# Block 0's retrieval made token-major by accumulating products, its first expert products cut by token halves, and the last block's second memory layer put among the experts

## The reference, cut to what matters

```python
# x: 2048 tokens (8 x 256) of 128 features
def lmm(params, h):                        # the memory, two layers
    for W, b in params:
        h = h + silu(h @ W + b)
    return h
# attention part: gradients of a weighted squared error of lmm(keys) against values,
# one Adam-like step on W1, b1, W2, b2, then the retrieval with the new parameters
new = adamw(params, grads)
retrieved = lmm(new, queries)
x = x + layernorm(retrieved)
# expert part: z = layernorm(layernorm(x)) * g + b; logits = z @ rW + rb; top 2 of 8, softmax over them
hid   = gelu(z @ W1[e] + b1[e])            # 128 -> 256, exact gelu
mixed = sum_e w[e] * (hid @ W2[e] + b2[e])
x = x + layernorm(layernorm(x) + mixed)
```

## Time and profile before

| | us |
|---|---|
| median of three runs | 188.84 |
| lowest, highest | 187.68, 188.96 |
| the profiled execution, device time | 187.79 |
| its span | 186.0 |
| TensorE products busy, of the span | 168.9 |
| VectorE busy | 137.1 |
| ScalarE busy | 95.4 |
| GpSimd busy | 25.2 |

### The profile page before, as it was taken

One profiled execution on the slowest core, in us unless ns is written; L12 is line 12 of the kernel. 1 busy time (PEld: TensorE's weight loads), 2 busy tenths in 40 slices (PEclk: granted clock), 3 DMA queues, 4 the chain that ended last, 5 costly groups with the idle time before them and its releaser, 6 DMA issues.

```text
span 186.0 us, 3109 instructions
## 1 busy us (share of the span) xinstructions
PE 168.9 (91%) x1036; PEld 136.4 (73%) x1036; DVE 137.1 (74%) x541; ACT 95.4 (51%) x165; POOL 25.2 (14%) x36
## 2 busy tenths in 40 slices
PE   6589999998999798996999999999999999999950
PEld 6334455666655367995999998998999998989940
DVE  0989998997766828399356979866979775458574
ACT  3059776765575597242725435725426725346300
POOL 1450000000031700024000025100026000002011
PEclk9999999999999999999999999999999999999995
DMA  4991000000000000000000000100000100000101
GB/s 140 310 314 42 5 4 0 0 0 2 4 0 0 0 0 2 4 0 0 0 4 0 2 0 4 56 0 0 5 0 0 59 2 0 0 4 2 56 0 56
DMA packets 3423, 4.99 MB, mean 27 GB/s; under 512 B 336, under 2 KB 1744, under 8 KB 3408
## 3 DMA queue, kind: packets, MB, share of 16 engines
q1 hardware_dynamic: 3408, 4.81, 8.2%
HBM read 3.76 MB, written 1.05 MB: 26 GB/s over the span
## 4 chain that ended last, share of the span: by engine, by line
PE 72%; DVE 17%; ACT 3%; issue 2%; DMA 2%; POOL 1%; SPq 0%; DVEq 0%; ACTq 0%
PE bank L372 66%; PE bank L380 4%; DVE stats L831 3%; DMA x_tok<-in_x_dram 2%; DVE xnT L1083 2%; DVE mv L834 1%; DVE xn_tok L988 1%; PE bank L525 1%; DVE xn_tok L844 1%; PE bank L516 1%; DVE h_tok L844 1%; ACT L753 1%; DVE xnT L1094 1%; DVE xnT L1114 1%; DVE xnT L1066 1%
## 5 line engine op out<-in xcount | busy, mean ns | idle before, releaser
L1083 DVE SCALAR_TENSOR_TENSOR xnT<-bank,w_tok,xnT 128x128 f32<-128x128 f32 x124 | 34.9, 345 | 24.4 <-PE bank L372 23.8
L325 POOL TENSOR_TENSOR rstd<-vpe,minus_half 128x4 f32<-128x4 f32 (+1 forms) x24 | 21.8, 913 | 116.5 <-DVE vpe L839 105.3
L372 PE MATMUL bank<-z_hi,fW_hi 128*128 128x512 f32 x64 | 27.8, 434 | 0.3 <-ACT alrT L649 0.3
L372 PE MATMUL bank<-z_hi,fW_lo 128*128 128x512 f32 x64 | 25.0, 390 | 0.0
L372 PE MATMUL bank<-z_lo,fW_hi 128*128 128x512 f32 x64 | 25.0, 393 | 0.0
L372 PEld LDWEIGHTS bank<-fW_sb,sig 128*128 128x128 f32 x192 | 23.0, 192 | 0.7
L372 PE MATMUL bank<-fW_sb,sig 128*128 128x128 f32 x192 | 23.2, 275 | 0.0
L772 ACT ACTIVATE sig<-bank,early_sb 128x512 f32<-128x512 f32 x24 | 16.1, 687 | 10.5 <-PE bank L372 10.4
L372 PEld LDWEIGHTS bank<-fW_sb,k_tok 128*128 128x128 f32 x160 | 19.4, 191 | 0.8
L372 PEld LDWEIGHTS bank<-fW_sb,h1T 128*128 128x128 f32 x160 | 19.4, 191 | 0.8
L372 PE MATMUL bank<-fW_sb,k_tok 128*128 128x128 f32 x160 | 19.5, 275 | 0.0
(11 more groups left out here) (128 smaller groups left out, 266.9 us busy)
## 6 DMA issues: line engine op xcount, KB each, us to landing
x_tok<-in_x_dram SPq DMA_DIRECT2D x4, 256.0 KB, 4.3
fW_raw<-in_fW_dram SPq DMA_DIRECT2D x1, 1024.0 KB, 9.8
out_dram<-xn_tok SPq DMA_DIRECT2D x3, 256.0 KB, 2.5
early_sb<-in_early_dram SPq DMA_DIRECT2D x1, 268.0 KB, 3.8
late_sb<-in_late_dram SPq DMA_DIRECT2D x1, 264.0 KB, 4.7
b_raw<-in_late_dram SPq DMA_DIRECT2D x16, 4.0 KB
out_dram<-xn_tok SPq DMA_DIRECT2D x2, 128.0 KB, 1.9
fW_sb<-in_fW_dram SPq DMA_DIRECT2D x1, 0.5 KB, 12.1
```

What stands on the lines that cost most here:

```text
L325: pool.tensor_tensor(rstd[:, ln, where], vpe[:, ln, where], minus_half[:, 0:where.stop - where.start], ALU.pow).then_inc(rstd_ready[ln], 1)
L372: return pe.matmul(out_, lhsT, rhs, start=start, stop=stop)
L1083: last = dve.scalar_tensor_tensor(out=y_tok[:, t, :], in0=bank[Y_BANK[m % len(Y_BANK)]][:, i * P:(i + 1) * P], scalar=w_tok[:, t, e:e + 1] ...
```

## The change

1. The Silu table is loaded by a dummy activation ahead of ScalarE's copy k(3), in the learning part, and no longer behind it.
2. Block 0 (pieces 0 and 1): no `retrieved_sum` and no transposes. `token_major_hidden` multiplies each tile of h1, as the stationary operand, with the identity into `R_BANK`, and `token_major_rest` adds the tile of s2 in the same way.
3. The rz products wait for qT block by block, rz1(2) is done in two halves, and the order on TensorE and ScalarE is another. `rz2_rest(3)` stands inside `first_hidden`.
4. `first_hidden` makes three hidden products (n = 0, 1, 2) in place of two, each by token halves: the z_hi products of the first half wait for the first half of z_hi only. All six z_lo products come behind.
5. The last piece's rz2 is one product, in slot 6 behind `output(6)`, in bank 4; its silu is made in slot 7 on ScalarE by x/2 (Identity) and tanh(x/2), which come from the Gelu table's set, and a product on VectorE (`last_product`) in slot 15. `hidden_sum(3)` and `(4)` move to slot 3.
6. `w_transpose(0)` stands behind `output(0)`, no longer ahead of it.
7. neg_shift and the L1 variance step leave `residual` for `residual_rest`, behind both `norm_z` of block 0 and directly behind `residual` of the later blocks. GpSimd does LZ of piece 1 ahead of L1 of piece 0.

```diff
-        RZ1, RZ2 = (3, 5, 7, 5, 6), (6, 2, 3, 2, 6)
-        R_BANK, Z_BANK = (4, 0, 4, 4, 4), (7, 1, 7, 7, 7)
+        RZ1, RZ2 = (3, 5, 7, 5, 6), (6, 2, 3, 2, 4)
+        R_BANK, Z_BANK = (4, 0, 4, 4, 4), (7, 6, 7, 7, 7)
+        HIDDEN_SUM, LAST_RZ2, LAST_TANH = 3, 6, 7
...
             piece_rsqrt(LZ, 0)
+            piece_rsqrt(LZ, 1)
             piece_rsqrt(L1, 0)
-            piece_rsqrt(LZ, 1)
...
+            def token_major_hidden(p):
+                pe.wait_ge(rh1_done, p + 1)
+                for i, t in enumerate(piece_tiles(p)):
+                    mm(bank[R_BANK[p]][:, i * P:(i + 1) * P], r_h1T[:, t * P:(t + 1) * P], ident[:],
+                       start=(i == 0), stop=False)
+
+            def token_major_rest(p):
+                pe.wait_ge(rs2_ready, p + 1)
+                for i, t in enumerate(piece_tiles(p)):
+                    last = mm(bank[R_BANK[p]][:, i * P:(i + 1) * P], r_s2[:, t * P:(t + 1) * P], ident[:],
+                              start=False, stop=(i == HALF - 1))
+                last.then_inc(r_tr, 1)
...
             rz1_product(1)
-            rz1_product(2)
+            rz1_part(2, slice(0, HALF * P), False)
             rz2_product(0)
+            token_major_hidden(0)
             rz2_product(1)
+            token_major_rest(0)
+            token_major_hidden(1)
+            token_major_rest(1)
+            rz1_part(2, slice(HALF * P, BLOCK), True)
+            rz1_product(3)
             rz2_query(2)
-            r_transpose(0)
-            r_transpose(1)
-            rz1_product(3)
+            rz2_rest(2)
             rz1_product(4)
+            z_transpose(0)
             rz2_query(3)
-            rz2_rest(2)
-            rz2_rest(3)
-            z_transpose(0)
-            rz2_query(4)
             z_transpose(1)
-            rz2_rest(4)
...
             def first_hidden():
+                halves = [slice(h * HALF * P, (h + 1) * HALF * P) for h in range(2)]
                 pe.wait_ge(x1_ready, 2)
...
+                for h, where in enumerate(halves):
+                    pe.wait_ge(zhi_done, h + 1)
+                    for n in range(len(H_BANK)):
+                        if h == 0 and n == 2:
+                            pe.wait_ge(rs1_ready, 4)
+                        s = slice(n * P, (n + 1) * P)
+                        mm(bank[H_BANK[n]][:, where], fW1_hi[:, s], z_hi[:, where], start=(h == 0), stop=False)
+                        mm(bank[H_BANK[n]][:, where], fW1_lo[:, s], z_hi[:, where], start=False, stop=False)
+                rz2_rest(3)
+                for h, where in enumerate(halves):
+                    pe.wait_ge(zlo_done, h + 1)
+                    for n in range(len(H_BANK)):
+                        last = mm(bank[H_BANK[n]][:, where], fW1_hi[:, n * P:(n + 1) * P], z_lo[:, where],
+                                  start=False, stop=(h == 1))
+                        if h:
+                            last.then_inc(h_mm, 1)
...
                 if slot == 0:
-                    w_transpose(0)
                     pe.wait_ge(fw2_in, 16)
-                    pe.wait_ge(rs2_ready, len(RETRIEVED))
+                    pe.wait_ge(rs2_ready, 4)
+                    pe.wait_ge(zT_ready, 2)
...
                 if slot >= 0:
                     output(slot)
+                if slot == 0:
+                    w_transpose(0)
+                if slot == LAST_RZ2:
+                    rz2_product(len(RETRIEVED) - 1)
...
+                    if (what, b) == ("k", NB - 1):
+                        act.activation(warm[:], minus_half[:, 0:1], ACT.Silu).then_inc(table_ready, 1)
...
-            act.activation(warm[:], minus_half[:, 0:1], ACT.Silu).then_inc(table_ready, 1)
+            def last_silu():
+                p = len(RETRIEVED) - 1
+                act.wait_ge(rz2_mm, p + 1)
+                act.wait_ge(half_bias, 1)
+                act.activation(nsig1[:, 0:BLOCK], bank[RZ2[p]][:], ACT.Identity, scale=0.5,
+                               bias=bn_half[:]).then_inc(halved, 1)
+                act.activation(nsig2[:, 0:BLOCK], bank[RZ2[p]][:], ACT.Tanh, scale=0.5,
+                               bias=bn_half[:]).then_inc(tanh_ready, 1)
+
...
             silu1(3)
+            silu2(2)
             silu1(4)
-            silu2(2)
-            silu2(3)
             zT_out(0)
             zT_out(1)
-            silu2(4)
+            silu2(3)
...
+            def last_product():
+                dve.wait_ge(halved, 1)
+                dve.wait_ge(tanh_ready, 1)
+                dve.scalar_tensor_tensor(out=piece(r_s2, len(RETRIEVED) - 1), in0=nsig2[:, 0:BLOCK], scalar=1.0,
+                                         in1=nsig1[:, 0:BLOCK], op0=ALU.add, op1=ALU.mult).then_inc(last_s2_done, 1)
...
+            def residual_rest(p):
+                where = piece_span(p)
+                plus_eps(L1, where)
                 dve.scalar_tensor_tensor(out=neg_shift[:, where], in0=mv[:, LR_, where, 0], scalar=-1.0,
                                          in1=rstd[:, LR_, where], op0=ALU.mult,
                                          op1=ALU.mult).then_inc(shift_ready, 1)
...
             hidden_sum(1)
-            retrieved_sum(0)
-            retrieved_sum(1)
...
             norm_z(1)
+            residual_rest(0)
+            residual_rest(1)
...
+                if slot == HIDDEN_SUM:
+                    half_of_bias()
+                    hidden_sum(3)
+                    hidden_sum(4)
```

More of the change, by code:

```diff
@@ L139, in memory_and_experts @@
         bn = sb("bn", [P, 2])
+        bn_half = sb("bn_half", [P, 1])
         stats = sb("stats", [P, T, 6])
@@ L190, in memory_and_experts @@
             "shift_ready", "centred", "lg_read", "dp_done"))
+        half_bias, halved, tanh_ready, last_s2_done = (sem(n) for n in (
+            "half_bias", "halved", "tanh_ready", "last_s2_done"))
         h_mm, g_done, y_mm, b2_mm, init_done, acc_done, yn_done = (sem(n) for n in (
@@ L478, in _, with rz1_part @@
                         steps[what](b)
-            def rz1_product(p):
+            def rz1_part(p, where, last):
                 if p == 0:
                     pe.wait_ge(w1n_ready, 1)
-                pe.wait_ge(qT_ready, NB)
+                pe.wait_ge(qT_ready, max(p, 1))
                 if p == 3:
@@ L488, in rz1_product @@
                     pe.wait_ge(rs2_ready, 1)
-                mm(bank[RZ1[p]][:, 0:piece_width(p)], w1n[:], piece(qT, p)).then_inc(rz1_mm, 1)
+                ins = mm(bank[RZ1[p]][:, where], w1n[:], piece(qT, p)[:, where])
+                if last:
+                    ins.then_inc(rz1_mm, 1)
+            def rz1_product(p):
+                rz1_part(p, slice(0, piece_width(p)), True)
             def rz2_product(p):
@@ L494, in rz2_product @@
                     pe.wait_ge(dh1_done, NB)
+                if p == 1:
+                    pe.wait_ge(qT_ready, NB)
+                if p == 4:
+                    pe.wait_ge(lg_read, 2)
                 pe.wait_ge(rh1_done, p + 1)
@@ L520, in z_transpose @@
                 pe.wait_ge(zt_ready, p + 1)
+                if p == 1:
+                    pe.wait_ge(rs1_ready, 5)
                 if p >= 2:
@@ L580, in hidden @@
                     pe.wait_ge(zlo_done, j + 2)
-                if n == C:
-                    pe.wait_ge(rs1_ready, 4)
                 if n >= len(H_BANK):
@@ L623, in _ @@
                 elif slot + AHEAD < STEPS:
-                    for c in range(C):
-                        hidden(C * (slot + AHEAD) + c)
+                    for n in range(C * (slot + AHEAD), C * (slot + AHEAD) + C):
+                        if n >= len(H_BANK):
+                            hidden(n)
                 if slot == 0:
-                    w_transpose(0)
                     pe.wait_ge(fw2_in, 16)
-                    pe.wait_ge(rs2_ready, len(RETRIEVED))
+                    pe.wait_ge(rs2_ready, 4)
+                    pe.wait_ge(zT_ready, 2)
                 if slot == 1:
@@ L788, in _ @@
                     gate_tanh(0)
+                if slot == LAST_TANH:
+                    last_silu()
                 if slot == 0:
@@ L991, in residual @@
                 last.then_inc(x1_ready, 1)
-                dve.scalar_tensor_tensor(out=neg_shift[:, where], in0=mv[:, LR_, where, 0], scalar=-1.0,
-                                         in1=rstd[:, LR_, where], op0=ALU.mult,
-                                         op1=ALU.mult).then_inc(shift_ready, 1)
                 yield
@@ L1001, in residual @@
                                   ALU.mult, ALU.add).then_inc(vpe_ready[LZ], 1)
+            def residual_rest(p):
+                where = piece_span(p)
                 plus_eps(L1, where)
+                dve.scalar_tensor_tensor(out=neg_shift[:, where], in0=mv[:, LR_, where, 0], scalar=-1.0,
+                                         in1=rstd[:, LR_, where], op0=ALU.mult,
+                                         op1=ALU.mult).then_inc(shift_ready, 1)
             def norm_z(p):
@@ L1139, in _ @@
```

(13 more changed lines are left out.)

16 lines of the change are left out of this document (10 added, 6 removed).

## The result

The changed kernel takes 0.7% longer than the one before: ratio 1.007, 95% interval 1.0048 to 1.0092. The medians of twenty executions each are 189.79 us (188.56 to 191.56) and 187.89 us (187.56 to 190.16), 1.0% apart; the ratio is one of means and leaves out executions that are more than 1.5% above the fastest of their kernel, here the one of 191.56. Both kernels' times stand in clusters, and the mean granted TensorE clock that each execution lists tells them apart.

| mean granted clock | executions | median us |
|---|---|---|
| 0.988 and more | 8 | 188.6 |
| 0.979 to 0.982 | 11 | 190.1 |
| 0.969 | 1 | 191.6 |

What follows compares the result with a forecast made beforehand. From 87 us TensorE's unbroken product list was taken to bound the kernel. Slot 1's -0.49, +0.07 for neg_shift and +0.86 for rz2_product(4) gave +0.44 us, 188.8 counted from 188.3; range 187.2 to 190.3.

Steps and rivals of the forecast that it cites:

- Silu load in its gap, at no price: Ahead of k(3)'s copy on ScalarE: load and dummy, 1.40 us, fit a 1.68 us idle gap and cost nothing.
- Rival D: Slower: the Silu load misses its gap and delays k(3)'s copy by 1.40 us; 190.1 us, chance 0.08.
- hidden_sum(0) at 55.35, rz2(0) at 55.93: Start of block 0's retrieval: silu1(0) starts 0.65 us earlier, then hidden_sum(0) at 55.35, rz2(0) at 55.93, silu2(0) at 56.63.
- Token-major products: Block 0's retrieval: transposes and two VectorE sums go, eight products come; VectorE's statistics start at 57.97, 0.82 us earlier.
- The decisive step, rz2_rest(3) ahead of the Gelu load: First expert products: silu2(3) waits for rz2_rest(3), first Gelu 0.64 us later, TensorE idle 1.5 us; 0.6 of 2.3 us lead left.
- The bound that I put behind it, retrieved_sum(2): Before slot 1: r_transpose(2) needs retrieved_sum(2), ending 74.32, so TensorE comes at 74.45; rival B has it hold r_transpose(2) too.
- rival B: Faster: the Gelu gate doesn't hold TensorE; slot 1 starts 1.15 us earlier, total -0.2, 188.1 us, chance 0.15.
- rz2_product(4) paid in full: Unbroken product list: rz2_product(4), two records of 0.43, adds 0.86 us with nothing to hide it.
- The wait for norm_z(2) stays, the rest is hidden: Block 1's z transposes: TensorE's 1.8 us wait moves along unchanged; added ScalarE steps and later sums cost nothing.
- slot 1's -0.49: After block 0's retrieval and first expert products: slot 1 starts 0.49 us earlier than in the kernel before.
- Rival C, the clock: Slower: waits of 0.98 and 1.5 us within 8 us lower TensorE's clock; +0.44 + 3.2, 191.9 us, chance 0.07.

Runs made afterwards that it cites:

- run 2: Changed kernel with GpSimd's two output-bias steps moved behind z_low(1): 188.2 us at a full clock, ratio 1.0060 to the kernel before.
- run 9: Kernel before with dummy transposes in two early TensorE waits, plus only the Silu load moved ahead of k(3)'s copy: 187.7 us, ratio 0.9987 to the kernel before.
- run 10: Kernel before with early dummy transposes, Silu load moved and GpSimd's bias steps behind z_low(1): 187.1 us at a full clock, ratio 0.9995 to the kernel before.
- run 4: Changed kernel with rz2_query(3) ahead of z_transpose(0) and rz2_rest(3) between the z transposes, out of first_hidden: 187.0 us at a full clock, ratio 0.9971 to the kernel before.
- run 5: Changed kernel with the last piece's rz2 as query and rest in slot 3, its silu in slot 4: 187.85 us at a full clock, ratio 0.9991 to the kernel before.
- run 8: Changed kernel with dummy transposes in the early TensorE waits and 12 in the wait for the first Gelu: 189.1 us, ratio 1.0029 to the kernel before.
- run 6: Kernel before with 4 more warm-up dummy transposes and 6 behind the first x transposes: 187.8 us at a full clock, ratio 0.9937, no falls in 12.
- run 3: Changed kernel with 12 dummy transposes in TensorE's wait for the first Gelu: 188.9 us without a fall, nine of twelve with one, ratio 1.0097 to the kernel before.

## Why the prediction was wrong, step by step

The forecast was +0.44 us and 188.8, read as no change, with slower by over 1% at 0.13. At a full clock it came to +0.9, and with the falls the medians are 1.9 us apart. Two steps failed: the price of hidden_sum(0), which took away what the new order was to gain, and the argument that let the clock stay up. That 189.79 lies inside the stated range, 187.2 to 190.3, is luck: the range had left the falls out, and they are what carries the median there. It is luck too that 188.8 is close to the 188.6 of a full clock: the 188.3 it counted from lay halfway between the two kinds of execution of the kernel before (187.7 and 189.1), 0.6 too high, and the change was put 0.5 too low.

- **Silu load in its gap, at no price.** Right. Load at 44.40, dummy right behind it at 45.69, copy not delayed. The Trainium skill (ScalarE: Activation LUTs, "What ACT_TABLE_LOAD costs") adds a drain of 1.38 us to every switch. The trace shows it at neither load: each begins 0.02 us behind the activation ahead of it (68.82 behind 68.80, for the Gelu one) and the next activation 0.01 behind its end. Rival D is out.
- **"hidden_sum(0) at 55.35, rz2(0) at 55.93".** This is the step that failed at a full clock. The sum started at 55.22 but took 1.1 us in place of the 0.43 of the earlier trace rows, because GpSimd was reading in its bias step until 56.05. Runs 2 and 9 show it from both sides: with GpSimd's step away the sum is short in the changed kernel, and with the load moved alone it gets long in the kernel before. The row was a price for a sum with GpSimd beside it for its first 0.15 us only. In all three profiles, of the kernel before, the changed one and run 9, the first sum ends 0.28 to 0.29 us behind GpSimd's step (56.43, 56.34 and 56.22), whether it had taken 0.43, 1.11 or 0.98. The Trainium skill (SBUF — State Buffer, "Who interferes with whom") has the rule: a VectorE `tensor_tensor` with both inputs in SBUF contends with GpSimd's reads, and which of the two blocks the other goes by the order of issue. The trace agrees: GpSimd's step began first (54.79) and took its usual 1.26 us, and the sum waited. I had looked at the VectorE queue for what the earlier start would collide with, and not at GpSimd's.
- **Token-major products.** The forecast's 0.82 stood for them and the load together; less the load's 0.65 it leaves them 0.17. Run 10 against run 2 gives them 0.15 us.
- **The decisive step, rz2_rest(3) ahead of the Gelu load.** Right in mechanism: a new TensorE wait for the first Gelu (1.3 us for 1.5 forecast). Run 4 prices the placement at 1.6 us. The bound that I put behind it, retrieved_sum(2), moves with the gates, so rival B's price was too low as well: it had slot 1 at most 1.15 us ahead of the kernel before, and in run 4 it is 1.46 ahead (measured from w1n's store to b2_term(0), 21.28 for 22.74), with the wait for the first Gelu not even gone (0.5).
- **rz2_product(4) paid in full.** Right: 0.86 forecast, 0.8 measured by run 5, and 1.72 us of it free in slot 3.
- **The wait for norm_z(2) stays, the rest is hidden.** Right: 1.8 us, and no new wait behind it.
- **The sum at a full clock.** The term that was mis-sized is slot 1's -0.49. In run 8's profile, where nothing falls, b2_term(0) starts at 77.20, and w1n's store ends at 54.33; in the kernel before it was 76.75 and 54.01. So the distance is 22.87 us for 22.74: slot 1 comes 0.1 us later where 0.49 earlier was forecast. With 0.07 and 0.86 that makes +1.0, for +0.9 measured. (Its dummies delay nothing here: hidden(3) starts 0.74 us behind the first Gelu with them, 71.27 behind 70.53, as without, 70.85 behind 70.11.) The rows, two of run 8 and one of the kernel before:

```profile
54.04 0.29 DVE L976 SCALAR_TENSOR_TENSOR w1n<-early_sb,adam_tmp 128x128 f32<-128x128 f32 x1
...
77.20 0.39 PE L376 MATMUL bank<-b_diag,wT 128*128 128x512 f32 x1
...
76.75 0.39 PE L372 MATMUL bank<-b_diag,wT 128*128 128x512 f32 x1
```

- **Rival C, the clock, at 0.07.** This is what failed for the median. The mechanism and the place (from the wait for the first Gelu on) were right; the argument against it was not. It read one execution of the kernel before, in which a wait of 1.8 us left the clock at 1.00, as a property of the kernel. For that wait the reading held up in runs 6 and 9 (24 executions), but not in run 10, and it didn't carry over to the new wait, shorter than 1.8 us as it is. Whether a given wait brings the clock down differs from execution to execution; a page of one shows one draw. The median of three in front of the prediction, 188.84 beside a lowest of 187.68, already held two kinds. The price was also off: 1.4 to 1.5 us, not 3.2. The stretch was 3.4 us at half speed, which by that costs at most 1.7 (an estimate), and not one in which 3.2 us of products take twice as long.

Left open: why the wait for norm_z(2) brings falls in run 10 and none in runs 6 and 9, why run 2 has more falls than the changed kernel, and the 0.4 to 0.6 us that the fills cost the changed kernel.

## What to carry to other kernels

When an edit moves a VectorE sum of two SBUF tensors, look at what GpSimd does at the new time, not at the old one: here it swallowed nearly the whole gain of a table load taken off the path. A function table's load should follow the last use of the old one at once; a product that this last use waits for belongs ahead of the work that has time. TensorE's idle stretches of one to two microseconds are worth filling, with real products where there are some. Dummies took the falls away too, free of charge in the kernel before and for 0.4 to 0.6 us in the changed one, so they are to be measured each time. In how many of the executions the clock falls shows in the list of executions and not in one profile.

## What the runs showed that I had not expected

- TensorE's waits between short bursts from 7 to 10 us (2.1 and 0.8 us in the profile of the kernel before) bring the clock to 1.2 GHz in about two fifths of the executions of the kernel before (39 of 93 had a fall, none of 12 with these waits filled; its own profile caught none, those of runs 3 and 4 did), and cost 1.2 to 1.4 us each time. Ten dummy transposes take that away: 187.8 for 188.2 in the median, none of 12 above 188.0.
- A VectorE sum of 256 columns, 0.43 us alone, takes 1.1 us when it starts in the middle of a GpSimd `tensor_tensor` of 1.26 us.
- A wait of 1.9 us can leave the clock alone in twelve executions of one kernel and bring it down in six of twelve of another that reaches it half a microsecond earlier.
